# Shared stage of an attention and mixture-of-experts kernel: routed rows added inside the group, its own product added block by block, the held token group moved to second place, and its first loads issued earlier

## The chip, the cores and the metric

The kernel runs on one core of one Trainium2 chip. The metric is the device time of one execution in microseconds (us), lower is better. The kernel before takes 2059.78 us (median of three runs, 2058.6 to 2061.94).

## The reference

The input `x` is 16 x 256 x 512 float32: 16 batches of 256 tokens with 512 features. A masked attention layer with 8 heads makes a tensor of the same shape, and a feed-forward layer with experts works on its rows, 4096 tokens in all. Cut to what matters for this change:

```
x = x + _L0_ffn_ref(_L0_cond_ref(x, cond_2048, Wq, Wo), ...)

def _L0_ffn_ref(x, gate_w, w_gate, w_up, w_down, sw_gate, sw_up, sw_down, shared_gate_w):
    E, K = (8, 2); I = 352; IS = 1408
    top_w, top_i = jax.lax.top_k(softmax(x @ gate_w.T), K)
    moe_out = sum over the 2 chosen experts of top_w * ((silu(x @ w_gate) * (x @ w_up)) @ w_down)
    sh = silu(x @ sw_gate) * (x @ sw_up)
    shared_out = sh @ sw_down
    return moe_out + shared_out * sigmoid(x @ shared_gate_w)
```

So each of the 4096 output rows is the input row, plus two routed rows with their weights, plus the row of the shared expert times its gate.

## The kernel before

The program has three stages, each a block of its own with a barrier of all engines between them. Every engine's instruction order is written out by hand, and semaphores tie the engines together; an engine works strictly in order, and SyncE (SP in the profile) issues nearly all DMAs, also in order. Full float32 products are made of three fast ones: each operand is split into a high and a low part (ScalarE makes the high part, VectorE the low one), and three matmuls add up high x high, high x low and low x high.

**Attention** writes its rows to `attn` in HBM, and the router's logits to SBUF. This change leaves it alone.

**Experts** (`experts`) begins with the up part of the shared expert for tokens 0 to 511, the *held* group. For t = 0 to 10 (11 slices of 128 of the 1408 hidden features) SP loads a slice of the weights (`load_up`), TensorE makes gate and up, and SP stores the result to `held` (line 755). VectorE sorts the tokens by expert in the meantime. Then each of the 8 experts works through its tiles of 256 slots: GpSimd gathers the rows (`gather`, line 826), TensorE turns them and makes gate and up (line 1138) and down (line 1150), ScalarE copies the result to `y` (line 901) and SP stores it to `routed` (line 769). SP loads the raw weights of expert 0 at the start, those of expert 1 with `load(1)` after the last `held` store, and later ones two experts ahead (lines 733 to 735). ScalarE splits the weights of expert 1 (`split(1, ...)`, line 846) before it takes up the first tile of expert 0, so the SiLU of that tile stands behind `load(1)`. When its loop is over SP issues `load_ahead` for the next stage (one DMA of 1024 KB for 512 rows of `attn`, six of 256 KB for the first two weight slices), waits for the last routed store, and goes to the barrier.

**Shared** (`shared`) works on groups of 512 tokens in four blocks of 128 rows. Groups 0 to 6 are tokens 512 to 4095, and the held group comes last. A full group has 11 steps t: gate and up products (`up`, line 1456, 12 matmuls each), SiLU, h split into halves (lines 1388, 1390), and `down` (line 1467, 12 matmuls into the four banks `ps_y`), one step behind. The rows of the next group are turned by TensorE (`turn`, line 1450) in the last step. The held group needs no gate and up: its 11 steps are a load of h from `held` into one of two buffers `h_up` (line 1295), two splits (lines 1402, 1404) and `down`. In group 0 each step also splits a weight slice (lines 1341 to 1342 and 1371 to 1373), and SP loads the slices two steps ahead (lines 1171, 1172).

The output of a block is put together in `total[s]`, which SP fills with the residual rows of `x` (line 1281). `add_down` (line 1419) adds the shared product when all of the group's products are done; `add_chosen` (lines 1427, 1430) then adds the two routed rows, in steps 0 to 3 of the *next* group, and SP stores the block (line 1285). The routed rows come through `chosen`, two pairs of buffers: GpSimd gathers those of block b (line 1326, two indirect DMAs) when block b - 2 is finished. After the last group `add_chosen` runs by itself. GpSimd also makes the stage's own identity matrix `ident` (lines 1309, 1311), for which TensorE waits at the start.

Of the kernel before, what the change touches and what calls it, by code (L numbers as in the profile page):

```python
# [586 lines left out]
def experts(nc, ctx, sems, keep, attn, w_gate, w_up, w_down, sw_gate, sw_up, held, routed):  # L587
# [7 lines left out]
    P = 128  # L595
# [24 lines left out]
    ident = sb("ident", [P, P], f32)  # L620
# [12 lines left out]
    y = sb("y", [P, SB, H], f32)  # L633
# [42 lines left out]
    y_done, stored = sem("y_done"), sem("stored")  # L676
# [53 lines left out]
    def _(sp):  # L730
# [444 lines left out]
def shared(nc, ctx, sems, keep, x, attn, sw_gate, sw_up, sw_down, held, routed, out):  # L1175
# [12 lines left out]
    HELD = 1  # L1188
    NG = NTOK // GT - HELD
    TOPK = 2  # L1190

# [9 lines left out]
    ident = sb("ident", [P, P], f32)  # L1201
# [9 lines left out]
    h_up = [sb(f"h_up{n}", [P, GT], f32) for n in range(2)]  # L1211
    h_in = [sem(f"h_in{n}") for n in range(2)]
# [4 lines left out]
    base, consts = sem("base"), sem("consts")  # L1217
# [3 lines left out]
    t_mm, g_mm, u_mm, y_mm = sem("t_mm"), sem("g_mm"), sem("u_mm"), sem("y_mm")  # L1221
    xhi_done, xlo_done = sem("xhi_done"), sem("xlo_done")
    silu_done, h_done, hhi_done, h_split = sem("silu_done"), sem("h_done"), sem("hhi_done"), sem("h_split")
    slot_done, scale_done, y_read, sum_done, out_ready = sem("slot_done"), sem("scale_done"), sem("y_read"), sem("sum_done"), sem("out_ready")
# [15 lines left out]
    def groups(eng, group):  # L1240

        group(0)
        with eng.Fori(1, NG - 1) as g:
            group(g)
        group(NG - 1)

    def more(g):
        return not isinstance(g, int) or g + 1 < NG

    def rows_of(g, s):  # L1250

        return (GB * (g + HELD) + s) * P if not isinstance(g, int) or g < NG else s * P

    def blocks_of(g):

        return bass.ds(GB * (g + HELD), GB) if not isinstance(g, int) or g < NG else slice(0, GB)

# [3 lines left out]
    def _(sp):  # L1261

        for t in range(2, NI):

            sp.wait_ge(w_lo, 2 * (t - 1))
            load_chunk(sp, keep["ahead"], sw_gate, sw_up, sw_down, t)

        def group(g):
            if more(g):

                sp.wait_ge(t_mm, HT * (g + 1))
                load_rows(sp, keep["ahead"], attn, g + 1 + HELD)
            if not isinstance(g, int) or g:
                store(g - 1)
            for s in range(GB):
                load_residual(g, s)

        def load_residual(g, s):

            upto(sp, stored[s], 16 * g)  # L1280
            sp.dma_start(total[s][:], x_v[bass.ds(rows_of(g, s), P), :]).then_inc(residual_in[s], 16)  # L1281

        def store_block(g, s):
            sp.wait_ge(out_ready, GB * g + s + 1)
            sp.dma_start(out_v[bass.ds(rows_of(g, s), P), :], total[s][:]).then_inc(stored[s], 16)

        def store(g):
            for s in range(GB):
                store_block(g, s)

        def load_held(t):
            if t >= 2:

                sp.wait_ge(h_split, NI * NG + t - 1)
            sp.dma_start(h_up[t % 2][:], held[t * P:(t + 1) * P, :]).then_inc(h_in[t % 2], 16)

        groups(sp, group)
        for t in range(NI):
            load_held(t)
            if 0 <= t - 2 < GB:  # L1300
                store_block(NG - 1, t - 2)
                load_residual(NG, t - 2)
# [273 lines left out]
```

## Time and profile before

| | |
|---|---|
| median of 3 runs | 2059.78 us |
| the profiled execution's own time | 2059.99 us |
| its span, first to last instruction | 2058.2 us |
| TensorE busy | 1922.2 us, 93% of the span |
| VectorE busy | 1082.7 us, 53% |
| ScalarE busy | 709.4 us, 34% |
| GpSimd busy | 620.0 us, 30% |
| mean granted TensorE clock | 0.964 of full speed |
| DMA | 195.83 MB, mean 95 GB/s |

The stages in time: attention to about 735 us, the up part of the held group to about 834, experts to about 1335, shared to the end. PE is TensorE's matmuls, PEld its weight loads, DVE VectorE, ACT ScalarE, POOL GpSimd and SPq SyncE's DMA issues. The share of busy time is an average over the three stages; what a change in one stage is worth is read from the waits in it. The granted clock has two levels, 1.00 (2.4 GHz) and 0.50 (1.2 GHz).

### The profile page before, as it was taken

What the parts mean: (1) busy time and instruction counts of PE and PEld (TensorE: products, weight loads), DVE (VectorE), ACT (ScalarE), POOL (GpSimd) and SP (SyncE); (2) the same over time, 40 slices, a digit from 0 to 9 for tenths busy, and PEclk for the clock granted to TensorE, in tenths of its full rate; (3) what the DMA queues carried; (4) which work ended last, traced back from release to release, by engine and by line L of the source; (5) the groups of instructions that cost most, each with busy time, mean ns of one, the idle gap of its engine ahead of it and who ended that gap; (6) DMA issues with size and microseconds to landing.
All of it is one profiled execution on the core that took longest, in us unless ns stands there. A gap on an engine that the chain in (4) does not pass through costs nothing. (4 is left out here: it accounts for less than half of the span.)

```text
span 2058.2 us, 30150 instructions
## 1 busy us (share of the span) xinstructions
PE 1922.2 (93%) x10324; PEld 1416.7 (69%) x10325; DVE 1082.7 (53%) x1723; ACT 709.4 (34%) x1276; POOL 620.0 (30%) x444
## 2 busy tenths in 40 slices
PE   4999999999999869899999999979999999999995
PEld 2444444444444347799999999868888888888874
DVE  3788878887888548443444433343423323242334
ACT  1566666666666623232333332231010101011000
POOL 3556566666665526211111111100101001010101
PEclk6899999999999969999999999989999999999998
DMA  7776767676765063422333232162302112130204
GB/s 125 111 115 100 111 96 130 101 108 98 128 90 73 21 226 97 150 91 100 124 124 111 83 115 82 67 182 73 102 21 82 41 61 66 36 102 0 93 26 143
DMA packets 117831, 195.83 MB, mean 95 GB/s; under 512 B 11264, under 2 KB 43008, under 8 KB 117776
## 3 DMA queue, kind: packets, MB, share of 16 engines
q1 hardware_dynamic: 106736, 158.94, 34.4%
q0 software_dynamic: 11040, 36.18, 6.1%
q8 instruction: 31, 0.51, 0.1%
q14 instruction: 24, 0.20, 0.0%
HBM read 100.68 MB, written 43.25 MB: 70 GB/s over the span
## 5 line engine op out<-in xcount | busy, mean ns | idle before, releaser
L420 DVE TENSOR_REDUCE maxcol<-ps_m 128x1 f32<-128x512 f32 x512 | 336.9, 681 | 138.5 <-PE ps_m L562 133.4
L337 ACT ACTIVATE e<-ps_e 128x512 f32<-128x512 f32 x512 | 297.3, 596 | 186.5 <-PE ps_e L557 185.7
L148 POOL TENSOR_TENSOR e<-e 128x2048 f32<-128x2048 f32 x64 | 225.6, 3524 | 179.0 <-ACT e L337 178.9
L1384 DVE TENSOR_TENSOR s_h_f<-s_silu,s_ps_u 128x512 f32<-128x512 f32 x77 | 52.9, 688 | 393.5 <-PE s_ps_u L1456 344.0
L562 PE MATMUL ps_m<-kside,qside 97*128 97x512 f32 x512 | 224.3, 443 | 34.7 <-DVE maxcol L420 19.1
L1326 POOL DMA_INDIRECT s_chosen<-routed,s_slot_now x64 | 61.6, 962 | 620.9 <-DVE s_total L1430 609.6
L557 PE MATMUL ps_e<-qside,kside 98*128 98x512 f32 x512 | 236.8, 465 | 3.3 <-ACT e L337 2.1
L557 PEld LDWEIGHTS ps_e<-qside,kside 98*128 98x128 f32 x512 | 96.8, 190 | 191.8 <-ACT e L337 158.7
L1352 ACT ACTIVATE s_silu<-s_ps_g 128x512 f32<-128x512 f32 x77 | 46.0, 598 | 528.8 <-PE s_ps_g L1456 521.3
L1053 DVE TENSOR_TENSOR e_h_f<-e_silu,e_ps_h 128x256 f32<-128x256 f32 (+1 forms) x108 | 45.2, 418 | 250.1 <-ACT e_silu L894 250.1
L562 PEld LDWEIGHTS ps_m<-kside,qside 97*128 97x128 f32 x512 | 101.1, 197 | 80.6 <-DVE maxcol L420 54.6
L1467 PE MATMUL s_ps_y<-s_d_hi,s_h_hi 128*128 128x512 f32 x352 | 140.0, 398 | 10.2 <-DVE s_h_lo L1404 10.2
L1467 PE MATMUL s_ps_y<-s_d_lo,s_h_hi 128*128 128x512 f32 x352 | 138.7, 394 | 0.0
L1467 PE MATMUL s_ps_y<-s_d_hi,s_h_lo 128*128 128x512 f32 x352 | 138.7, 394 | 0.0
L455 PE MATMUL ps_num<-e,v 128*32 128x512 f32 x1024 | 138.0, 611 | 0.1
L386 DVE RECIPROCAL den<-den 128x128 f32<-128x128 f32 x128 | 119.5, 940 | 15.4 <-ACT den L268 15.4
L1456 PE MATMUL s_ps_g<-s_x_hi,s_gu_hi 128*128 128x512 f32 x308 | 121.3, 394 | 3.7 <-DVE s_d_lo L1373 3.6
L1138 PE MATMUL e_ps_h<-e_x_hi,e_hi_g 128*128 128x256 f32 (+1 forms) x432 | 122.0, 282 | 1.7 <-DVE e_x_lo L917 1.7
L1138 PE MATMUL e_ps_h<-e_x_lo,e_hi_u 128*128 128x256 f32 (+1 forms) x432 | 121.9, 282 | 0.0
L1138 PE MATMUL e_ps_h<-e_x_lo,e_hi_g 128*128 128x256 f32 (+1 forms) x432 | 121.9, 282 | 0.0
L1138 PE MATMUL e_ps_h<-e_x_hi,e_lo_g 128*128 128x256 f32 (+1 forms) x432 | 121.8, 282 | 0.0
L1138 PE MATMUL e_ps_h<-e_x_hi,e_hi_u 128*128 128x256 f32 (+1 forms) x432 | 121.6, 281 | 0.0
(233 smaller groups left out, 4189.0 us busy)
## 6 DMA issues: line engine op xcount, KB each, us to landing
routed<-e_y SPq DMA_DIRECT2D x36, 512.0 KB, 2.8
kside<-q_hi SPq DMA_DIRECT2D x64, 256.0 KB
qside<-qm_hi SPq DMA_DIRECT2D x64, 256.0 KB
x_f<-in_x SPq DMA_DIRECT2D x16, 512.0 KB, 3.5
kside<-q_lo SPq DMA_DIRECT2D x32, 256.0 KB
qside<-qm_lo SPq DMA_DIRECT2D x32, 256.0 KB
attn<-xo SPq DMA_DIRECT2D x32, 256.0 KB, 3.4
keep_rows<-attn SPq DMA_DIRECT2D x8, 1024.0 KB, 5.6
```

Source lines behind the costliest of these rows:

```text
L148: eng.tensor_tensor(into, into, e[k + 1][:, heads, :], ALU.add).then_inc(done, 1)
L337: act.activation(e[kb][:, g, :], ps_e[g % 2][:, :], ACT.Exp, scale=SCALE).then_inc(e_done, 1)
L386: dve.reciprocal(den[par][:, c], den[par][:, c]).then_inc(rd_done, 1)
L420: dve.reduce_max(maxcol[par][:, g * KB + kb:g * KB + kb + 1], ps_m[g % 2][:, :], AX.X).then_inc(max_done, 1)
L455: last = nc.tensor.matmul(ps_num[g * DK:(g + 1) * DK, :], v[n % RING][:, kb, g, :], e[kb][:, g, :], start=(kb == 0), stop=(kb == KB - 1))
L557: nc.tensor.matmul(ps_e[g % 2][:, :], kside[n][:, g, cols], qside[n][:, g, :], start=True, stop=True).then_inc(e_mm, 1)
L562: nc.tensor.matmul(ps_m[g % 2][:, :], qside[s2][0:MAXROW, g, cols], kside[s2][0:MAXROW, g, :], start=True, stop=True).then_inc(m_mm, 1)
L1138: last = nc.tensor.matmul(ps_h[t][0:width, k, :], l[k][:, m, at:at + width], r[:, m, :], start=(c == 0), stop=(c == len(terms) - 1))
L1326: pool.indirect_dma_start(out=chosen[k][s % 2][:], out_offset=None, in_=routed, in_offset=bass.IndirectOffsetOnAxis(ap=slot_now[:, k, s:s ...
L1384: dve.tensor_tensor(h_f[:], silu[:], ps_u[:], ALU.mult).then_inc(h_done, 1)
L1456: last = nc.tensor.matmul(ps[:], l[:, t, k, m, :], r[:, m, :], start=(c == 0), stop=(c == len(terms) - 1))
L1467: last = nc.tensor.matmul(ps_y[s][:], l[t % 2][:, c], r[:, t, :], start=(t == 0 and m == 0), stop=(t == NI - 1 and m == 2))
```

## The change

- The held group is at place 1, after one full group (tokens 512 to 1023), and six full groups follow. The function `places` sets this order for all engines. Its h goes through three buffers, two of which are the two halves of `y`, the buffer of the experts' results, which is now kept alive.
- `add_chosen` runs in steps 5 to 8 of the group's own 11 steps (`ADD_AT` = 5), before the shared product is there; a new semaphore `chosen_used` frees the `chosen` buffers. `add_down` comes at the end, block by block: TensorE signals each of the first three blocks by `y_last`, and the store of a block follows it.
- The copies of the weights (`scales`) stand at the start of a group.
- SP issues `load_ahead` before `load(1)` in the experts stage, right after the last `held` store. At the end of that stage SP does not wait for the routed stores any more; GpSimd does so at the start of the shared stage, before the first gather.
- In the shared stage SP issues the loads for the second full group's rows, the residual rows and the first three held slices after weight slice 3, before slice 4. The order before had rows and residual behind slice 10.
- `ident` is made once, in the experts stage.

The core of the diff:

```diff
@@ experts, SyncE
             sp.wait_ge(a_h_done, t + 1)
             sp.dma_start(held[t * P:(t + 1) * P, :], a_h[t % 2][:]).then_inc(a_stored[t % 2], 16)
+        sp.wait_ge(a_wlo, SI)
+        sp.wait_ge(a_t_mm, HT)
+        keep["load_ahead"](sp)
         sp.wait_ge(lo_done, NPARTS)
         load(1)
...
         each_expert(sp, start, tile)
-        total = sp.value_load(keep["bounds"][0:1, NE:NE + 1], min_val=1, max_val=NTILES - 1)
         for n in range(2):
             sp.wait_ge(a_stored[n], 16 * ((SI - n + 1) // 2))
-        keep["load_ahead"](sp)
-        alone(sp, stored, 16 * total + 16, consts, 8)
@@ shared
+    ADD_AT = NI - GB - 2
...
+    RING = 3
+    y = keep["ahead"]["y"]
+    h_up = [y[:, 0, :], y[:, 1, :], sb("h_up", [P, GT], f32)[:]]
...
+    def places(eng, group, held_group, alone_too=0):
 
         group(0)
-        with eng.Fori(1, NG - 1) as g:
-            group(g)
+        held_group()
+        for p in range(HELD_AT + 1, HELD_AT + 1 + alone_too):
+            group(p)
+        with eng.Fori(HELD_AT + 1 + alone_too, NG - 1) as p:
+            group(p)
         group(NG - 1)
@@ shared, SyncE
+        def exchange(p):
+            for s in range(GB):
+                if not isinstance(p, int) or p:
+                    store_block(p - 1, s)
+            for s in range(GB):
+                load_residual(p, s)
+
+        def load_held(t):
+            if t >= RING:
+
+                sp.wait_ge(h_split, NI * HELD_AT + t - RING + 1)
+            sp.dma_start(h_up[t % RING], held[t * P:(t + 1) * P, :]).then_inc(h_in[t % RING], 16)
...
+        def group_held():
+            exchange(HELD_AT)
+            for t in range(RING, NI):
+                load_held(t)
+
         for t in range(2, NI):
 
             sp.wait_ge(w_lo, 2 * (t - 1))
             load_chunk(sp, keep["ahead"], sw_gate, sw_up, sw_down, t)
...
+            if t == 3:
+                group(0)
+                sp.wait_ge(slot_done, 1)
+                for k in range(RING):
+                    load_held(k)
@@ shared, GpSimd
-        pool.memset(ident[:], 0.0).then_inc(base, 1)
-        pool.wait_ge(base, 1)
-        pool.affine_select(out=ident[:], in_=ident[:], compare_op=ALU.not_equal, fill=1.0, base=0,
-                           pattern=[[-1, P]], channel_multiplier=1).then_inc(consts, 1)
...
+        written = pool.value_load(keep["bounds"][0:1, NE:NE + 1], min_val=1, max_val=keep["tiles"] - 1)
+        alone(pool, keep["routed_stored"], 16 * written + 16, t_mm, 1)
...
-                    alone(pool, out_ready, b - 1, consts, 1)
+                    alone(pool, chosen_used, b - 1, slot_done, 1)
@@ shared, VectorE
+        def add_down(p):
+
+            dve.wait_ge(chosen_used, GB * (p + 1))
+            for s in range(GB):
+                if s < GB - 1:
+                    dve.wait_ge(y_last, (GB - 1) * p + s + 1)
+                else:
+                    dve.wait_ge(y_mm, NI * (p + 1))
+                dve.scalar_tensor_tensor(out=total[s][:], in0=ps_y[s][:], scalar=scale_now[:, TOPK, s:s + 1],
+                                         in1=total[s][:], op0=ALU.mult, op1=ALU.add).then_inc(out_ready, 1)
...
+        def group_held():
+            scales(HELD_AT)
+            for t in range(NI):
+                dve.wait_ge(h_in[t % RING], 16 * (t // RING + 1))
+                halves(HELD_AT, t, h_up[t % RING])
+                if ADD_AT <= t < ADD_AT + GB:
+                    add_chosen(HELD_AT, t - ADD_AT)
+            add_down(HELD_AT)
@@ shared, TensorE
-        pe.wait_ge(consts, 1)
...
+                if t == NI - 1 and s < GB - 1:
+                    last.then_inc(y_last, 1)
             last.then_inc(y_mm, 1)
```

**How the order moves, at three places.** On SP in the experts stage, between the last stores of `held` and the weights of expert 1 (`e_raw_*`), one piece of the difference (+ is the change):

```order
 L755 DMA held<-e_a_h 128x512 x3
+L1163 DMA keep_rows<-attn 128x4x512
+L1171 DMA keep_raw_gu<-in_sw_gate 128x4x128
+L1171 DMA keep_raw_gu<-in_sw_up 128x4x128
+L1172 DMA keep_raw_d<-in_sw_down 128x512
+L1171 DMA keep_raw_gu<-in_sw_gate 128x4x128
+L1171 DMA keep_raw_gu<-in_sw_up 128x4x128
+L1172 DMA keep_raw_d<-in_sw_down 128x512
 L733 DMA e_raw_g<-in_w_gate 128x4x352
 L733 DMA e_raw_u<-in_w_up 128x4x352
```

Seven DMAs of the next stage now stand ahead of `load(1)`; before, nothing did.

On SP in the shared stage of the change, between weight slices 3 and 4 (`keep_y` and `s_h_up` are the three held buffers, `s_total` the residual):

```order
L1171 DMA keep_raw_gu<-in_sw_up 128x4x128
L1172 DMA keep_raw_d<-in_sw_down 128x512
L1163 DMA keep_rows<-attn 128x4x512 [waits s_t_mm]
L1273 DMA s_total<-in_x 128x512 x4
L1290 DMA keep_y<-held 128x512 [waits s_slot_done]
L1290 DMA keep_y<-held 128x512
L1290 DMA s_h_up<-held 128x512
L1171 DMA keep_raw_gu<-in_sw_gate 128x4x128 [waits s_w_lo]
```

Eight DMAs, 2816 KB, now stand ahead of slice 4; before, slice 4 followed slice 3 at once.

On VectorE, the end of the program; before:

```order
L1419 SCALAR_TENSOR_TENSOR s_total<-s_ps_y,s_scale_now,s_total 128x512 [waits s_residual_in3]
L1427 SCALAR_TENSOR_TENSOR s_total<-s_chosen,s_scale_now,s_total 128x512 [waits s_y_read,s_chosen_in0]
L1430 SCALAR_TENSOR_TENSOR s_total<-s_chosen,s_scale_now,s_total 128x512 [waits s_sum_done]
L1427 SCALAR_TENSOR_TENSOR s_total<-s_chosen,s_scale_now,s_total 128x512 [waits s_y_read,s_chosen_in1]
L1430 SCALAR_TENSOR_TENSOR s_total<-s_chosen,s_scale_now,s_total 128x512 [waits s_sum_done]
L1548 UNCONDITIONAL_BRANCH
```

and in the change:

```order
L1391 CAST s_h_hi<-s_h_f 128x512 [waits s_y_mm,s_h_done]
L1393 TENSOR_TENSOR s_h_lo<-s_h_f,s_h_hi 128x512 [waits s_hhi_done]
L1422 SCALAR_TENSOR_TENSOR s_total<-s_ps_y,s_scale_now,s_total 128x512 [waits s_y_last,s_chosen_used]
L1422 SCALAR_TENSOR_TENSOR s_total<-s_ps_y,s_scale_now,s_total 128x512 [waits s_y_last] x2
L1422 SCALAR_TENSOR_TENSOR s_total<-s_ps_y,s_scale_now,s_total 128x512 [waits s_y_mm]
L1574 UNCONDITIONAL_BRANCH
```

The eight additions of routed rows (two for each block) that followed the last product are gone from the end, and only one addition waits for the very last product (`s_y_mm`).

## Rows read from the trace of the kernel before

**Rows 1.** The page: busy time, share of the span and instructions of each engine.

```profile
PE 1922.2 (93%) x10324; PEld 1416.7 (69%) x10325; DVE 1082.7 (53%) x1723; ACT 709.4 (34%) x1276; POOL 620.0 (30%) x444
```

**Rows 2.** Chain that ended last: the last down step of full groups; start, us, what.

```profile
1522.68 2.72 PE s_ps_y L1467 x12
...
1890.11 2.72 PE s_ps_y L1467 x12
```

**Rows 3.** Busy time by stretch: us, each engine, granted clock, DMA share, GB/s.

```profile
1538.40:1630.00 91.60, 91.60 (x412) 75.68 (x412) 30.89 (x51) 8.86 (x15) 7.86 (x9) 1.00 0.17 56
...
1995.50:2041.40 45.90, 35.65 (x133) 27.71 (x132) 20.76 (x36) 0.00 (x0) 8.76 (x9) 0.89 0.44 143
2041.40:2058.20 16.80, 0.03 (x1) 0.00 (x0) 8.56 (x12) 0.00 (x0) 4.05 (x4) 0.61 0.39 125
```

**Rows 4.** Timeline of SP and POOL at the end of experts: start, us, [idle before <-releaser].

```profile
1336.13 0.37 SPq L769 DMA_DIRECT2D routed<-e_y  x1
1337.32 0.40 SPq L1163 DMA_DIRECT2D keep_rows<-attn  x1
...
1341.53 1.59 SPq L1172 DMA_DIRECT2D keep_raw_d<-in_sw_down  x1
...
1343.71 0.21 POOL L1309 MEMSET s_ident<- 128x128 f32 x1 [22.82 <-POOLq L1546]
```

**Rows 5.** Timeline of PE from there to the first product of shared.

```profile
1344.43 1.97 PE L1450 MATMUL s_ps_t<-s_ident,keep_rows 128*128 128x128 f32 x8 [9.11 <-POOL s_ident L1311]
...
1352.51 0.76 PE L1456 MATMUL s_ps_g<-s_x_hi,s_gu_hi 128*128 128x512 f32 x1 [3.58 <-DVE s_d_lo L1373]
```

**Rows 6.** Timeline of SP, ACT and PE at the start of expert 0, around `load(1)`.

```profile
833.81 0.44 SPq L733 DMA_DIRECT2D e_raw_g<-in_w_gate  x1
...
844.44 1.38 ACT L846 ACTIVATE e_hi_g<-e_raw_g 128x1408 fp32r<-128x1408 f32 x1 [8.35 <-DMA e_raw_d<-in_w_down]
...
852.00 0.79 PE L1150 MATMUL e_ps_y<-e_hi_d,e_h_hi 128*128 128x512 f32 x1 [3.85 <-DVE e_h_lo L1057]
```

**Rows 7.** Busy time by stretch: `load(1)` moving, `load_ahead` moving.

```profile
837.00:840.00 3.00, 2.94 (x14) 2.95 (x14) 0.00 (x0) 0.00 (x0) 1.40 (x2) 0.50 1.07 393
...
1337.20:1346.00 8.80, 1.57 (x8) 1.57 (x8) 0.00 (x0) 0.42 (x1) 1.62 (x4) 0.58 1.04 309
```

**Rows 8.** A load behind a full queue at the start of experts; the zero fills' landing (DMA list).

```profile
753.33 1.17 SPq L739 DMA_DIRECT2D keep_raw_gu<-in_sw_gate  x1
...
764.63 1.06 ACT L861 ACTIVATE e_hi_g<-keep_raw_gu 128x1024 fp32r<-128x1024 f32 x1 [8.73 <-DMA keep_raw_gu<-in_sw_up]
...
routed<-e_zeros SPq DMA_DIRECT2D x9, 512.0 KB, 10.8
```

**Rows 9.** Group 0 of shared: ACT around weight slice 4.

```profile
1365.77 1.06 ACT L1341 ACTIVATE s_gu_hi<-keep_raw_gu 128x1024 fp32r<-128x1024 f32 x1 [2.33 <-DMA keep_raw_d<-in_sw_down]
...
1371.00 0.60 ACT L1352 ACTIVATE s_silu<-s_ps_g 128x512 f32<-128x512 f32 x1 [3.65 <-PE s_ps_g L1456]
```

**Rows 10.** The held group: waits of PE, VectorE's steps, the gather.

```profile
1999.50 0.50 PE L1467 MATMUL s_ps_y<-s_d_hi,s_h_hi 128*128 128x512 f32 x1 [3.93 <-DVE s_h_lo L1404]
...
1998.30 0.42 DVE L1402 CAST s_h_hi<-s_h_up 128x512 fp32r<-128x512 f32 x1
...
2000.14 0.75 DVE L1430 SCALAR_TENSOR_TENSOR s_total<-s_chosen,s_scale_now,s_total 128x512 f32<-128x512 f32 x1
...
2007.75 0.75 DVE L1427 SCALAR_TENSOR_TENSOR s_total<-s_chosen,s_scale_now,s_total 128x512 f32<-128x512 f32 x1 [2.58 <-DMA s_chosen<-routed,s_slot_now]
```

**Rows 11.** VectorE after the last product of group 0, and at the end of the program.

```profile
1446.63 2.73 DVE L1419 SCALAR_TENSOR_TENSOR s_total<-s_ps_y,s_scale_now,s_total 128x512 f32<-128x512 f32 x4 [1.35 <-issue]
...
2041.53 2.73 DVE L1419 SCALAR_TENSOR_TENSOR s_total<-s_ps_y,s_scale_now,s_total 128x512 f32<-128x512 f32 x4 [4.12 <-issue]
...
2054.96 0.75 DVE L1430 SCALAR_TENSOR_TENSOR s_total<-s_chosen,s_scale_now,s_total 128x512 f32<-128x512 f32 x1
```

**Rows 12.** DMA list, residual rows: KB each, median us from issue to landing.

```profile
s_total<-in_x SPq DMA_DIRECT2D x32, 256.0 KB, 4.3
```

More of the change, by code:

```diff
@@ L1238, in alone, with more, full, tokens @@
         eng.wait_ge(s, value)
-    def groups(eng, group):
+    def places(eng, group, held_group, alone_too=0):
         group(0)
-        with eng.Fori(1, NG - 1) as g:
-            group(g)
-        group(NG - 1)
[L1247 to L1256, printed above, removed]
+        held_group()
[3 more added lines that the diff above has]
+            group(p)
+        group(NG - 1)
+    def more(p):
+        return not isinstance(p, int) or p + 1 < NG
+    def full(p):
+        return 0 if isinstance(p, int) and p == 0 else p - 1
+    def tokens(p):
+        return {0: HELD_AT, HELD_AT: 0}.get(p, p) if isinstance(p, int) else p
     block = ctx.enter_context(nc.Block())
@@ L1266, in _ @@
             load_chunk(sp, keep["ahead"], sw_gate, sw_up, sw_down, t)
[L1268 to L1302, printed above, removed]
-        store(NG)
+            if t == 3:
[3 more added lines that the diff above has]
+                    load_held(k)
+        places(sp, lambda p: None if isinstance(p, int) and p == 0 else group(p), group_held, 1)
         for s in range(GB):
-            sp.wait_ge(stored[s], 16 * (NG + 1))
+            store_block(NG - 1, s)
@@ L1342, in split, with group @@
             act.activation(d_hi[:, t], raw_d[t % 2][:], ACT.Copy).then_inc(w_hi, 1)
-        def group(g):
-            first = isinstance(g, int) and g == 0
+        def group(p):
+            first = isinstance(p, int) and p == 0
+            f = full(p)
             for t in range(NI):
@@ L1373, in split @@
             dve.tensor_tensor(d_lo[:, t], raw_d[t % 2][:], d_hi[:, t], ALU.subtract).then_inc(w_lo, 1)
-        def group(g):
-            first = isinstance(g, int) and g == 0
-            for t in range(NI):
-                if first and t + 2 < NI:
-                    split(t + 2)
-                n = NI * g + t
-                dve.wait_ge(silu_done, n + 1)
-                dve.wait_ge(u_mm, n + 1)
-                upto(dve, h_split, n)
-                dve.tensor_tensor(h_f[:], silu[:], ps_u[:], ALU.mult).then_inc(h_done, 1)
-                dve.wait_ge(h_done, n + 1)
-                upto(dve, y_mm, n if t == 0 else n - 1)
-                dve.tensor_copy(h_hi[t % 2][:], h_f[:]).then_inc(hhi_done, 1)
-                dve.wait_ge(hhi_done, n + 1)
-                dve.tensor_tensor(h_lo[t % 2][:], h_f[:], h_hi[t % 2][:], ALU.subtract).then_inc(h_split, 1)
-                if t < GB and (not isinstance(g, int) or g):
-                    add_chosen(g - 1, t)
-            if more(g):
-                x_low(g + 1)
-            add_down(g)
@@ L1435, in _, with turn @@
         split(1)
-        groups(dve, group)
-        group_held()
-        for s in range(GB):
-            add_chosen(NG, s)
+        places(dve, group, group_held)
     @block.tensor
     def _(pe):
-        pe.wait_ge(consts, 1)
-        def turn(g, m):
+        def turn(f, m):
             if m == 0:
-                pe.wait_ge(rows_in, 16 * (g + 1))
-            upto(pe, xlo_done, HT * g + m - 1)
+                pe.wait_ge(rows_in, 16 * (f + 1))
+            upto(pe, xlo_done, HT * f + m - 1)
             for s in range(GB):
```

178 lines of the change are left out of this document (103 added, 75 removed).

## The prediction

> **What bounds the kernel now.** I read the page first: TensorE is busy 93% of the span, no other engine over 53% [rows 1], so what counts is where PE waits or runs at half clock. The chain of waits then shows the shared stage's full groups: the same down step recurs four groups later after 1890.11 - 1522.68 = 367.43 us, 91.86 us for each, without a gap [rows 2], and the stretch table has such a stretch filled, at granted clock 1.00 and a DMA share of 0.17 [rows 3]. Nothing is to be had there. The same table shows two stretches where PE is not filled: the held group, 45.90 us with 35.65 busy at clock 0.89, and 16.80 us behind it with no product at all [rows 3]. The timelines add two places. Between experts and shared PE idles 9.11 us until `ident` is made, and waits again before its first product [rows 5]; GpSimd makes `ident` only when SP, last at the barrier, has issued its seven loads [rows 4]. And at the start of expert 0, PE idles 3.85 us because ScalarE stood 8.35 us waiting for `load(1)` [rows 6]. That one is not a target of the change, but a moved step runs into it.
>
> **a. Seven loads ahead of `load(1)`.** They are 1024 + 6 x 256 = 2560 KB, 2.62 MB. `load(1)` began at 833.81 and its last piece released ScalarE at 844.44 [rows 6], 10.6 us, and in the middle of it the DMA engines were full and moved 393 GB/s [rows 7]. So time ahead of it is not absorbed: ScalarE splits expert 1's weights before the first SiLU of expert 0, VectorE's h stands behind that, PE's down behind h, and after 852.00 PE has no slack up to the end of the stage. The delay passes on one to one. Price: the same seven loads moved at 309 GB/s, a store included [rows 7], 2.62 MB / 309 = 8.5 us; at the 393 GB/s of `load(1)` it is 6.7 us. I take the middle, **+7.6 us**. Lower bound 4: the 6.4 us of a slightly better rate, less some of the half-clock time that PE has after its wait anyway. Upper bound 10.5: a weight slice that met a full queue released ScalarE at 764.63 after its issue at 753.33, 11.3 us, of which a DMA alone needs a part [rows 8]. The row shows that a load behind others lands late; it does not show that the queue is served in order. The Trainium skill, "DMA: Bandwidth & Descriptors", section "Queues, rings and completion order", says that each DMA engine consumes a queue's descriptors in ring order, which speaks against this part of the change. By its fabric ceiling of 435 GB/s ("Specifications") the term would be an estimated 6.0 us and the sum 1.6 us lower; the measured rates decide here.
>
> **b. From experts to shared.** SP's last store is issued by 1336.13 + 0.37 = 1336.50. Before, it went on to load, and its last issue ended at 1341.53 + 1.59 = 1343.12; GpSimd started 0.59 after [rows 4]. Now SP leaves the loop (at most the 0.8 us that lay before 1337.32) and reaches the barrier near 1336.7; 0.6 us later every engine goes, and PE needs no `ident`. PE starts near 1337.3 instead of 1344.43, **-7.1 us** (bounds -7.5 and -5.8). The wait for the last routed store moves to GpSimd; queued behind it are the slot copy and the first gathers, which nobody needs before step 5. The held loads on SP wait for that copy, too, long after it is done. From the first turn to the first product 8.08 us pass [rows 5]; the chain of ScalarE and VectorE in it stays, its 16 turns ran at half clock and may be quicker after a shorter idle time: **-0.5** (0 to -1.5).
>
> **c. Group 0.** SP puts eight DMAs, 2816 KB or 2.88 MB, ahead of slice 4. At 309 to 393 GB/s they take 7.3 to 9.3 us from about the time that slice 3 is through. Slice 4 was in at 1365.77, and would now be in near 1370; ScalarE splits it (1.06 us and a smaller piece) before SiLU 2, which began at 1371.00 [rows 9], and PE asks for SiLU 2 only after an up and a down product, 5.4 us later. The cover is about 4 us: **0**, and up to +4 if it is gone, since later slices catch up.
>
> **d. The held group at place 1.** Before, from the end of the last full group (1995.6) to the last product (2041.5, when VectorE starts [rows 11]) it took 45.9 us [rows 3]. Now, counted from the end B of group 0: VectorE, idle for 1.35 us before group 0's additions after the low parts of the next rows, is free from about B - 1.4, so its four additions, 2.73 us, end near B + 1.4 [rows 11]; the scale copies take 0.25, and from a finished addition to the first product took 1.1 us (split at 1998.30, product at 1999.50 [rows 10]). PE waits 2.75 us where it waited 3.93. Then 11 steps of 2.72 = 29.9 us [rows 2]. Stalls on `held` should go: three slices are there, and slice 3 comes behind the last store (2.5 us) and the residual loads that wait for the stores, so it is issued near B + 4.5 and lands some 4.3 later, as a residual load does [rows 12], and is needed by B + 9.7. A new stall comes: blocks 0 and 2 share a pair of buffers, and from a finished block to the next gather's arrival 2000.9 to 2007.75 = 6.85 us passed [rows 10], while here only two steps, 5.44 us, lie between. VectorE waits 3 us in step 7, and PE about 1.5 us in step 8. With 0.85 us for one possible half-clock stretch the group takes 2.75 + 29.9 + 1.5 + 0.85 = 35.0: **-10.9 us**. Bounds: -12.5 if the gather is covered and the clock holds, -7 with one more wait like the 3.93.
>
> **e. The end.** Before, 16.7 us from the last product to the end of the span. Now three blocks are added while the last one is multiplied; after it come one addition (0.75, and 0.1 to start) and one store. The last addition before ended at 2054.96 + 0.75 = 2055.71, 2.5 us before the end [rows 11]; three stores just ahead cost 0.2. That is 3.5 us: **-13.2 us** (-13.6 to -12).
>
> **Costed at nothing:** `add_chosen` in steps 5 to 8 of full groups (two additions, 1.5 us, in a step of 8.16 where VectorE is busy a third of the time [rows 3]; gathers have 16 us); `y_last`, an increment on a product that exists; two more scale copies ahead of splits.
>
> **The sum:** 7.6 - 7.1 - 0.5 + 0 - 10.9 - 13.2 = -24.1 us. Against the profiled execution's 2059.99 us that gives 2035.9; it lay 0.2 above the median of the runs, so I forecast **2035.7 us**, 1.2% faster. The bounds are rarely bad together; the case's own range is 2031 to 2042.
>
> **Rivals.** (1) *The early loads cost nothing*: `load(1)` overtakes them, or the wait is hidden. For it: a part of the 10.6 us is issue and start, which may overlap. Against it: ScalarE's 8.35 us wait was on the path, with full engines. Term a goes, 2035.7 - 7.6 = 2028.1. (2) *The held group keeps its stalls*: SP's chain of stores, residual loads and held loads, or the gather, costs as much at place 1 as at the end. For it: both showed as waits there. Against it: three slices are loaded far ahead. Term d goes, 2046.6. (3) *The boundary does not shrink*, so the change does not do what it says: something other than SP and `ident` holds PE, a barrier or code. Term b goes, 2043.3. Against it: GpSimd started 0.59 us after SP's last issue. (4) *Slower*: `load(1)` is served far later than the rates say. Its place is ScalarE's split before expert 0's first SiLU, and it decides from a delay of 7.6 + 24.1 = 31.7 us, at which the 2.62 MB move at under 83 GB/s. The nearest row for such a price is the zero fills, 10.8 us for 512 KB [rows 8]; five times that is 54 us, which gives 2035.7 - 7.6 + 54 = 2082. Against it: these landed late because they stood in line behind each other, at full rate.
>
> **How the numbers follow.** Forecast 0.76, rival 1 0.10, rival 2 0.08, rival 3 0.04, rival 4 0.02. The range of 8 in 10 runs from rival 1 up to near rival 3, 2028 to 2043; left out are rivals 2 and 4 and the tails of the forecast. A measurement of this kernel tells 0.2%, some 4 us, from no change. All cases but rival 4 lie far below that, so faster 0.97, same 0.01, slower 0.02.
>
> **What would show it.** a: ScalarE's wait before `e_hi_g` at the start of expert 0 is near 16 us instead of 8.35, PE's behind it near 11. b: PE idles some 2 us between the stages, and no `ident` is made. c: no PE wait at SiLU in group 0. d: PE waits near 2.8 us at the held group's first product, about 1.5 in step 8, and not on `held`. e: about 3.5 us from the last product to the end. The forecast is wrong if ScalarE's wait stays at 8 us, if PE waits on held slices at place 1, or if group 0 is longer than before.

## The result, and the profile after

The change takes the kernel from 2060.39 us (median of four runs, the three above and one more, 2058.6 to 2061.94) to **2045.47 us** (median of four, 2045.07 to 2046.97). The ratio is 0.9929, with a 95% interval of 0.9912 to 0.9946: 0.7% faster. The forecast was 2035.7 with a range of 2028 to 2043, so the direction was right, the gain was 14.9 us where 24.1 were forecast, and the time lies 2.5 us above the range. The profiled execution took 2045.46 us with a span of 2043.7, 14.5 below the span before.

The page after hardly differs from the one before [rows 1]:

```profile
PE 1920.0 (94%) x10324; PEld 1415.8 (69%) x10325; DVE 1080.5 (53%) x1723; ACT 709.3 (35%) x1276; POOL 619.9 (30%) x442
```

TensorE has the same work, and what changed are its idle and half-clock stretches. So the reading goes through the five places of the prediction. Timelines give the start, the duration, the instruction, and in brackets the idle time before it with its releaser.

**a, experts.** ScalarE and PE at the start of expert 0 (before: 8.35 and 3.85 us, [rows 6]):

```profile
855.27 1.38 ACT L846 ACTIVATE e_hi_g<-e_raw_g 128x1408 fp32r<-128x1408 f32 x1 [17.87 <-DMA e_raw_d<-in_w_down]
```
```profile
862.83 0.79 PE L1150 MATMUL e_ps_y<-e_hi_d,e_h_hi 128*128 128x512 f32 x1 [14.78 <-DVE e_h_lo L1057]
```

ScalarE waits 9.5 us longer and PE 10.9. From the first turn of expert 0 to the last product of the stage it took 501.08 us before (834.24 to 1335.32), and now 510.20 (835.56 to 1345.76): **+9.1**, with +7.6 forecast. The profiles of the runs below bear this out: in the six that have the seven loads ahead of `load(1)`, this one included, the stage takes 509.4 to 510.6 us, and in the four that have none ahead 498.9 to 501.1, on average 10.1 less. One pair is good to about a microsecond. SP shows why ScalarE waits:

```profile
835.21 0.38 SPq L1163 DMA_DIRECT2D keep_rows<-attn  x1
...
839.76 1.52 SPq L1172 DMA_DIRECT2D keep_raw_d<-in_sw_down  x1
841.33 0.44 SPq L733 DMA_DIRECT2D e_raw_g<-in_w_gate  x1
...
845.34 0.47 SPq L735 DMA_DIRECT2D e_raw_d<-in_w_down  x1
```

The seven early loads occupy SP from 835.21 to 841.28, and `load(1)` follows. Of `load(1)` the last piece is issued by 845.81 and in at 855.27. So 6.1 of the 9.5 us pass before `load(1)` is even issued. The stretch table shows the DMA engines full the whole time, and the DMA list has 1.05 MB of gathers by GpSimd in it beside the loads (columns: the stretch, its length, the busy time of PE, PEld, DVE, ACT and POOL, the granted clock, the DMA share, GB/s):

```profile
835.60:855.30 19.70, 10.73 (x88) 10.26 (x88) 1.29 (x2) 1.11 (x3) 4.21 (x6) 0.87 0.97 310
```

**b, the boundary.** PE idles 1.88 us where it idled 9.11 [rows 5]: **-7.2**, with -7.1 forecast.

```profile
1347.64 1.06 PE L1467 MATMUL s_ps_t<-keep_ident,keep_rows 128*128 128x128 f32 x8 [1.88 <-PEq L1572]
...
1355.23 0.76 PE L1473 MATMUL s_ps_g<-s_x_hi,s_gu_hi 128*128 128x512 f32 x1 [3.58 <-DVE s_d_lo L1385]
```

From the first turn to the first product it is 7.59 us where it was 8.08, the forecast **-0.5**, and for the reason that it named: the first eight turns take 1.06 us where they took 1.97 [rows 5]. All eight profiles with 1.9 us of idle time have 7.6 us here, and the three with 4.8 us or more have 8.1.

**c, group 0.** From its first product to its end 95.81 us pass, before 94.04: **+1.8**, with 0 forecast. ScalarE waited 6.91 us for weight slice 2 (before 5.10) and 7.88 for slice 4 (before 2.33, [rows 9]). Only the first of these reaches PE. ScalarE before, its wait for slice 2, and then ScalarE and PE in the change:

```profile
1357.59 1.06 ACT L1341 ACTIVATE s_gu_hi<-keep_raw_gu 128x1024 fp32r<-128x1024 f32 x1 [5.10 <-DMA keep_raw_d<-in_sw_down]
```
```profile
1362.12 1.06 ACT L1352 ACTIVATE s_gu_hi<-keep_raw_gu 128x1024 fp32r<-128x1024 f32 x1 [6.91 <-DMA keep_raw_d<-in_sw_down]
1364.41 1.06 ACT L1352 ACTIVATE s_gu_hi<-keep_raw_gu 128x1024 fp32r<-128x1024 f32 x1 [0.23 <-DMA keep_raw_d<-in_sw_down]
1367.35 0.60 ACT L1364 ACTIVATE s_silu<-s_ps_g 128x512 f32<-128x512 f32 x1 [1.35 <-PE s_ps_g L1473]
1375.83 1.06 ACT L1352 ACTIVATE s_gu_hi<-keep_raw_gu 128x1024 fp32r<-128x1024 f32 x1 [7.88 <-DMA keep_raw_d<-in_sw_down]
```
```profile
1364.32 0.47 PE L1473 MATMUL s_ps_g<-s_x_hi,s_gu_hi 128*128 128x512 f32 x1 [1.67 <-ACT s_silu L1364]
```

**d, the held group** runs from 1451.04 to 1491.26, 40.2 us where it took 45.9 [rows 3]: **-5.7**, with -10.9 forecast. PE waits three times, never for `held`:

```profile
1453.79 0.50 PE L1484 MATMUL s_ps_y<-s_d_hi,s_h_hi 128*128 128x512 f32 x1 [2.75 <-DVE s_h_lo L1393]
1477.90 0.50 PE L1484 MATMUL s_ps_y<-s_d_hi,s_h_hi 128*128 128x512 f32 x1 [0.43 <-DVE s_h_lo L1393]
1483.88 0.50 PE L1484 MATMUL s_ps_y<-s_d_hi,s_h_hi 128*128 128x512 f32 x1 [2.95 <-DVE s_h_lo L1393]
```

and runs at half clock after the first and the third wait (1.00 would be 2.4 GHz, 0.50 is 1.2 GHz):

```profile
1451.00:1491.30 40.30, 34.17 (x134) 27.18 (x134) 21.39 (x38) 0.00 (x0) 8.71 (x9) 0.92 0.59 186
1454.70:1457.70 3.00, 3.00 (x8) 2.30 (x7) 0.10 (x1) 0.00 (x0) 0.00 (x0) 0.50 0.96 307
1484.90:1488.20 3.30, 3.30 (x10) 2.54 (x9) 0.07 (x1) 0.00 (x0) 2.18 (x3) 0.53 0.68 192
```

Its 11 steps are 29.9 us at full clock [rows 2]. PE was busy for 34.17, so the clock cost 4.3, some 2 for each stretch; the other 6.1 are the waits, 2.75 + 0.43 + 2.95. Behind the second and the third wait stands VectorE, which waits for gathered rows (L1408 adds the first of the two rows of a block):

```profile
1470.49 0.75 DVE L1408 SCALAR_TENSOR_TENSOR s_total<-s_chosen,s_scale_now,s_total 128x512 f32<-128x512 f32 x1
1471.27 0.75 DVE L1411 SCALAR_TENSOR_TENSOR s_total<-s_chosen,s_scale_now,s_total 128x512 f32<-128x512 f32 x1
1475.25 0.75 DVE L1408 SCALAR_TENSOR_TENSOR s_total<-s_chosen,s_scale_now,s_total 128x512 f32<-128x512 f32 x1 [1.95 <-DMA s_chosen<-routed,s_slot_now]
1476.03 0.75 DVE L1411 SCALAR_TENSOR_TENSOR s_total<-s_chosen,s_scale_now,s_total 128x512 f32<-128x512 f32 x1
1481.22 0.75 DVE L1408 SCALAR_TENSOR_TENSOR s_total<-s_chosen,s_scale_now,s_total 128x512 f32<-128x512 f32 x1 [3.37 <-DMA s_chosen<-routed,s_slot_now]
```

Block 0 is added by 1469.30 and block 2's rows are in at 1475.25, 5.95 us later. Block 1 is added by 1472.02 and block 3's rows are in at 1481.22, **9.2 us** later, though it is the same pair of gathers. GpSimd issues them directly one after the other, and SP issues the 1024 KB of rows for the next group in the same moment:

```profile
1472.36 1.03 POOL L1338 DMA_INDIRECT s_chosen<-routed,s_slot_now  x1 [0.30 <-DVE s_total L1411]
1473.69 0.94 POOL L1338 DMA_INDIRECT s_chosen<-routed,s_slot_now  x1 [0.30 <-issue]
```
```profile
1473.69 0.43 SPq L1163 DMA_DIRECT2D keep_rows<-attn  x1
```

It was no single event: in the six profiles that keep these steps and this row load, block 2's rows take 5.9 to 6.2 us and block 3's 9.0 to 10.2, PE's third wait is 2.6 to 3.7 us, and a half-clock stretch follows it each time.

**e, the end.** VectorE's four additions (before [rows 11]) now overlap the last products, and 3.4 us lie between the last product at 2040.3 and the end, before 16.8: **-13.4** beside -13.2 forecast.

```profile
2038.36 2.73 DVE L1422 SCALAR_TENSOR_TENSOR s_total<-s_ps_y,s_scale_now,s_total 128x512 f32<-128x512 f32 x4 [1.54 <-PE s_ps_y L1484]
```

The six full groups take 549.04 us beside 549.1 before. Expert 0's first turn came 1.3 us later, which the change isn't shown to cause: in its own profile and those of its eight variants, whose edits lie behind that point, the turn lies between 833.9 and 838.3. The sum: 1.3 + 9.1 - 7.2 - 0.5 + 1.8 - 5.7 - 13.4 = -14.6, the span's -14.5. The 9.6 us by which the forecast's -24.1 missed it are, in order of size, **d 5.2, c 1.8, a 1.5, the start 1.3**.

### The profile page after: what moved, and what is told of

Its sections match the earlier page's. It is cut to its first block and busy times, and to the rows that moved or that the text cites. A ratio compares the mean times of both kernels' runs of the same rounds, so it can differ in the third digit from the quotient of the medians.

```text
span 2043.7 us, 30248 instructions
## 1 busy us (share of the span) xinstructions
PE 1920.0 (94%) x10324; PEld 1415.8 (69%) x10325; DVE 1080.5 (53%) x1723; ACT 709.3 (35%) x1276; POOL 619.9 (30%) x442
## 3 DMA queue, kind: packets, MB, share of 16 engines
q1 hardware_dynamic: 106736, 158.94, 34.6%
## 5 line engine op out<-in xcount | busy, mean ns | idle before, releaser
L823 POOL COPY e_now<-e_token_of 128x2 uint32 (+1 forms) x37 | 7.2, 195 | 384.3 <-PE e_ps_t L1121 383.0
```

## The experiments

Unless said otherwise each is an edit of the changed kernel. Runs with one time have no interval; in those the trace at the place of the edit decides, not the total.

### Is the wait at expert 0 a matter of the order of SP's loads?

```diff
             sp.dma_start(held[t * P:(t + 1) * P, :], a_h[t % 2][:]).then_inc(a_stored[t % 2], 16)
+        sp.wait_ge(lo_done, NPARTS)
+        load(1)
         sp.wait_ge(a_wlo, SI)
         sp.wait_ge(a_t_mm, HT)
         keep["load_ahead"](sp)
-        sp.wait_ge(lo_done, NPARTS)
-        load(1)
```

> The changed kernel with load(1) issued before the seven early loads, everything else as in the change. Theory A (the seven loads delay load(1) by the time that their 2.62 MB take on the DMA engines, and that reaches TensorE one to one): ScalarE's wait before expert 1's split falls from 17.87 us back to about 8.4, TensorE's from 14.78 to about 3.9, and the kernel is 9.1 us faster than the change, near 2036.4. Theory B (the experts stage began 1.3 us late and the rest is the warm-up of the clock or another cause, not the place of the loads): less than 3 us gained. Theory C (whatever is second in the queue pays: the seven loads collide with the gathers and the loads of expert 2): TensorE's wait shrinks by 11 us, but part of it comes back within the experts stage or at its end.

Measured: 2035.55 us (median of four, 2033.65 to 2036.63), ratio to before 0.9879 (0.9862 to 0.9895). Timelines of ScalarE and of PE:

```profile
847.85 1.38 ACT L846 ACTIVATE e_hi_g<-e_raw_g 128x1408 fp32r<-128x1408 f32 x1 [8.62 <-DMA e_raw_d<-in_w_down]
```
```profile
855.40 0.79 PE L1150 MATMUL e_ps_y<-e_hi_d,e_h_hi 128*128 128x512 f32 x1 [5.54 <-DVE e_h_lo L1057]
```

ScalarE's wait is back at 8.6 us, though the same 2.62 MB now follow right behind `load(1)`, and the experts take 500.4 us (837.38 to 1337.78), 9.8 less than in the change. The total is 9.9 less, so nothing of it comes back elsewhere, as theory C had it. The boundary idle stays at 1.88. So the whole of a comes from the loads that stand ahead of `load(1)`; loaded behind it they are hidden, and b is kept.

### Which of the seven loads costs what?

Here only the 1024 KB of rows are ahead of `load(1)`, and the six weight loads behind it:

```diff
-        keep["load_ahead"](sp)
+        keep["rows_ahead"](sp)
         sp.wait_ge(lo_done, NPARTS)
         load(1)
+        keep["load_ahead"](sp)
```

> The changed kernel with only one of the seven loads, the rows (1024 KB, 1.05 MB), ahead of load(1), and the six weight loads (1536 KB) behind it. Theory A by bytes: TensorE's wait at expert 0 rises by 1.05 / 2.62 of the 10.9 us that it rose by, so it is near 8.2 us (3.85 + 4.4) instead of 14.78. Theory A by issue: a DMA's cost is its issue time on SyncE (0.4 us for the rows, 5.7 for the six), so the wait is near 4.5 us. If the 512-byte lines of the weight slices are the slow part, the rows cost 1.05 MB / 393 GB/s = 2.7 us and the wait is near 6.5.

Measured: 2040.85 us (one run). PE (one line further down than in the change):

```profile
838.26 1.09 PE L1122 MATMUL e_ps_t<-keep_ident,e_rows 128*128 128x128 f32 x8 [1.72 <-DMA e_rows<-attn,e_now]
...
859.13 0.79 PE L1151 MATMUL e_ps_y<-e_hi_d,e_h_hi 128*128 128x512 f32 x1 [6.88 <-DVE e_h_lo L1058]
```

PE's wait of 6.88 us lies nearest the 6.5 that the text above has for slow short lines. But the wait also takes in how fast PE ran before it, so the time from the first turn to the product after the wait is the better measure. It is 20.87 us here, 27.27 in the change, and 18.02 in the run before, with nothing ahead of `load(1)`. By these three profiles the rows (1.05 MB) cost 2.85 us and the six weight loads (1.57 MB) 6.4. Theory A by issue falls, since the rows take SP 0.4 us to issue.

Whether short lines make the weight loads slower (four of the six have lines of 512 bytes, the other two and the rows of 2048) isn't shown. The same time lies between 16.45 and 18.02 us in the four profiles with nothing ahead and between 26.47 and 27.39 in the six with all seven. Held against these, the rows cost 2.9 to 4.4 us (237 to 368 GB/s) and the weight loads 5.6 to 6.5 (241 to 281 GB/s), which overlap. From average to average it is 9.7 us for all seven, of which the rows take 3.6, and their share by bytes would be 3.9.

### What delays block 3's gather?

SP's load of the next rows waits until the routed rows of the held group are added:

```diff
                 sp.wait_ge(t_mm, HT * (full(p) + 1))
+                if isinstance(p, int) and p == HELD_AT + 1:
+                    sp.wait_ge(chosen_used, GB * (HELD_AT + 1))
                 load_rows(sp, keep["ahead"], attn, tokens(p + 1 if not isinstance(p, int) or p else HELD_AT + 1))
```

> The changed kernel with the load of the rows for the third full group held back on SyncE until the held group's routed rows are added. Theory D (block 3's gather, 9.2 us from a free buffer to its rows, is slow because that 1024 KB load was issued at the same time and shares the DMA engines): VectorE's wait of 3.37 us for it falls below 1 us, TensorE's wait of 2.95 us in the held group and the half-clock stretch behind it go, and the held group takes some 4 us less than its 40.2. Theory E (the two gathers of a pair of blocks stand behind each other on GpSimd and at the DMA, whatever else runs): the wait stays within 1 us of 2.95.

Measured: 2039.87 us (one run). VectorE:

```profile
1470.31 0.75 DVE L1413 SCALAR_TENSOR_TENSOR s_total<-s_chosen,s_scale_now,s_total 128x512 f32<-128x512 f32 x1
1474.55 0.76 DVE L1410 SCALAR_TENSOR_TENSOR s_total<-s_chosen,s_scale_now,s_total 128x512 f32<-128x512 f32 x1 [2.22 <-DMA s_chosen<-routed,s_slot_now]
1475.34 0.75 DVE L1413 SCALAR_TENSOR_TENSOR s_total<-s_chosen,s_scale_now,s_total 128x512 f32<-128x512 f32 x1
1477.08 0.75 DVE L1410 SCALAR_TENSOR_TENSOR s_total<-s_chosen,s_scale_now,s_total 128x512 f32<-128x512 f32 x1
```

Block 1 is added by 1471.06, block 3's rows are there without a wait at 1477.08, at most 6.0 us later, where it was 9.2. PE keeps its first wait and 0.70 us in step 8; the 2.95 us and the half-clock stretch behind it are gone. The group takes 35.6 us:

```profile
1450.11:1485.70 35.59, 32.14 (x133) 26.17 (x134) 21.22 (x37) 0.00 (x0) 8.79 (x9) 0.95 0.62 201
```

That is 4.6 us less than in the change: 2.7 in waits and 1.9 in clock. So the row load delays block 3's gather, and theory E falls. That 35.6 lies near the forecast's 35.0 is in part luck: the later wait is 0.70 us where 1.5 were forecast, and the one half-clock stretch costs 2.2 where 0.85 were.

### Or can the gather be given more time?

The four additions of the held group go into steps 3, 4, 8 and 9 instead of 5 to 8, so that five steps and not two lie between a pair of buffers' release and its next use. The row load stays where the change has it:

```diff
-                if ADD_AT <= t < ADD_AT + GB:
-                    add_chosen(HELD_AT, t - ADD_AT)
+                if t in (3, 4, 8, 9):
+                    add_chosen(HELD_AT, (3, 4, 8, 9).index(t))
```

> The changed kernel with the held group's routed rows added in steps 3, 4, 8 and 9 instead of 5, 6, 7 and 8. Both D and E: from block 0's addition to block 2's lie five steps, 13.6 us, more than the 9.2 us of the slower gather, so TensorE's waits of 0.43 and 2.95 us in the held group and the half-clock stretch behind them go, and the group takes 40.2 - 3.4 - 1.6 = 35.2 us. If the residual rows are not there by step 3, a wait for them in step 3 takes part of it back.

Measured: 2037.63 us (one run). The only wait left in the group is the one at its start, and the clock holds:

```profile
1453.21 0.50 PE L1484 MATMUL s_ps_y<-s_d_hi,s_h_hi 128*128 128x512 f32 x1 [2.74 <-DVE s_h_lo L1393]
```
```profile
1450.47:1483.40 32.93, 30.19 (x133) 25.01 (x134) 21.22 (x37) 0.00 (x0) 9.14 (x9) 1.00 0.68 224
```

32.9 us, 7.3 less than in the change. Of the 2.7 us between this and the run before, 0.7 are the wait in step 8; the rest is clock (30.19 busy against 32.14), and most of it came behind the wait at the group's start, 2.75 us in both, after which the clock fell in the one run and held in the other. So about 2 us of this are no effect of the edit. PE is busy for 30.19 us with no half-clock stretch, 32.14 with one and 34.17 with two.

### What makes the new wait in group 0?

First the transfers ahead of slice 4, two slices later:

```diff
-            if t == 3:
+            if t == 5:
                 group(0)
```

> The changed kernel with weight slices 4 and 5 issued before the eight loads (rows, residual, held) of SyncE's first group, instead of behind them. Theory F (TensorE's 1.67 us wait at the first SiLU of group 0 comes from those eight DMAs): the wait goes. Theory G (it comes from the four gathers, which now start 2.6 us after TensorE instead of together with it and run into slices 2 and 3): the wait stays between 0.6 and 1.7 us, ScalarE's wait for slice 4, 7.88 us, falls back to about 2.3, and since slice 4 was covered anyway, the kernel's time is within 1.5 us of the change's.

Measured: 2045.15 us (one run). ScalarE's wait for slice 4 falls from 7.88 to 0.48 us, and yet nothing is gained: PE's wait at SiLU is 2.25 us, ScalarE's for slice 2 is 7.39, and group 0 takes 97.9 us, 2.1 more than in the change. (The total comes out level since the clock held at the start of this run's held group.) So slice 4 was covered, as c had it, and the eight loads alone don't make the 1.8 us. Next the first gathers, held back until weight slice 2 is through:

```diff
             pool.wait_ge(slot_done, p + 1)
+            if isinstance(p, int) and p == 0:
+                pool.wait_ge(w_lo, 6)
```

> The changed kernel with the gathers of group 0 held back until weight slice 2 is split. Theory G: slices 2 and 3 have the DMA engines to themselves, ScalarE's wait for slice 2 falls from 6.91 us to about 4.5, TensorE's wait of 1.67 us at the first SiLU goes, group 0 is 1.7 us shorter. Theory F: the wait stays. The gathers now meet the eight loads and slice 4, whose cover was 3 us; if that is used up, a new wait at the third SiLU appears.

Measured: 2044.10 us (one run). PE's wait is 0.86 us, ScalarE's for slice 2 6.13, and group 0 takes 95.0, 0.8 less than in the change. ScalarE's wait for slice 4 grows to 9.60, and no wait at the third SiLU appears. That looks like an answer until it is held against the other six variants, which all have the early gathers and the eight loads: there the same PE wait is 0.58 to 1.11 us (0.81 with ScalarE's at 6.06). So the gathers alone aren't shown to be the cause either.

The wait itself is the change's, though. PE has it in all nine profiles of the change and its variants (0.58 to 2.25 us, ScalarE's for slice 2 5.5 to 7.5), and in neither profile of the kernel before, where ScalarE waits 4.7 and 5.1. Each suspect was taken away alone, never both together, so that either of them suffices isn't excluded. **Its cause stays open**, and c is worth 0.4 to 2.3 us (group 0 takes 94.4 to 96.4 in the eight profiles other than the run on slices 4 and 5).

### Is it SP's issuing that holds the boundary?

The seven loads back at the end of the experts stage, all else as in the change:

```diff
-        sp.wait_ge(a_wlo, SI)
-        sp.wait_ge(a_t_mm, HT)
-        keep["load_ahead"](sp)
         sp.wait_ge(lo_done, NPARTS)
         load(1)
...
             sp.wait_ge(a_stored[n], 16 * ((SI - n + 1) // 2))
+        keep["load_ahead"](sp)
```

> The changed kernel with the seven loads back at the end of the experts stage, identity matrix and the wait for the routed stores as in the change. Theory A: TensorE's wait at expert 0 is back near 4 to 5.5 us, 9 to 10 us gained there; at the boundary SyncE's 5.9 us of issue are back before the barrier, so TensorE idles about 1.9 + 6.6 = 8.5 us instead of 1.88. Net some 3 us faster than the change, near 2042. If SyncE's issue was not what held the barrier (rival 3 of the prediction), the idle time stays near 2 us and the kernel comes out near 2036.

Measured: 2037.10 us (one run). SP, and then PE (two lines further up):

```profile
1333.90 0.37 SPq L769 DMA_DIRECT2D routed<-keep_y  x1
1334.53 0.40 SPq L1161 DMA_DIRECT2D keep_rows<-attn  x1
...
1339.02 1.85 SPq L1170 DMA_DIRECT2D keep_raw_d<-in_sw_down  x1
```
```profile
1341.31 1.94 PE L1465 MATMUL s_ps_t<-keep_ident,keep_rows 128*128 128x128 f32 x8 [8.21 <-PEq L1570]
```

PE idles 8.21 us instead of 1.88 and starts 0.44 after SP's last issue, with no `ident` to wait for. The experts take 499.2 us, 11.0 less than in the change. So the early loads alone, in the place the change gives them, give 6.3 us at the boundary (and the 0.5 behind it) and take 11.0 at the start: **this part of the change costs more than it brings**. The total was expected near 2042 and came 5 lower: a is 11.0 here and not 9.1, the first turn came 1.65 earlier, and the held group took 1.7 less, since its first half-clock stretch did not come.

### The early loads without the rest of the change

This is the kernel *before* with only the seven loads moved ahead of `load(1)`. SP still waits for the routed stores at the end of the stage:

```diff
             sp.dma_start(held[t * P:(t + 1) * P, :], a_h[t % 2][:]).then_inc(a_stored[t % 2], 16)
+        sp.wait_ge(a_wlo, SI)
+        sp.wait_ge(a_t_mm, HT)
+        keep["load_ahead"](sp)
         sp.wait_ge(lo_done, NPARTS)
         load(1)
...
-        keep["load_ahead"](sp)
         alone(sp, stored, 16 * total + 16, consts, 8)
```

> The kernel before with one part of the change alone: the seven loads moved ahead of load(1). Everything else, the wait for the routed stores and the stage's own identity matrix included, stays. Theory A: TensorE's wait at expert 0 rises from 3.85 us to about 14, 9 to 10 us lost. At the boundary SyncE has no loads to issue, but still waits for the last routed store, which lands some 3 us after its issue, and GpSimd makes the identity matrix after that, so TensorE's idle time falls from 9.11 us only to about 5.5. Net some 6 us slower than the kernel before, near 2066: this part alone is a loss. If TensorE's wait at expert 0 depended on something else in the change, the kernel would be 3 to 4 us faster than before.

Measured: 2065.63 us (median of ten, 2063.27 to 2068.83) beside 2060.65 for the kernel before, ratio 1.0024 (1.0015 to 1.0034): **slower by 0.24%**, 5 us where 6 were forecast. PE's wait at expert 0 is 14.90 us, and at the boundary 4.81:

```profile
863.25 0.79 PE L1152 MATMUL e_ps_y<-e_hi_d,e_h_hi 128*128 128x512 f32 x1 [14.90 <-DVE e_h_lo L1059]
...
1350.54 1.97 PE L1452 MATMUL s_ps_t<-s_ident,keep_rows 128*128 128x128 f32 x8 [4.81 <-POOL s_ident L1313]
```

The boundary gives only 4.3 of its 9.11 us, since SP's last store is issued by 1346.91 and GpSimd makes `ident` only at 1349.82, 2.9 us later: the wait for that store, and the barrier. Moving this wait to GpSimd behind the barrier, and keeping `ident`, is what brings the idle time down to 1.88. No run separates the two; GpSimd starts `ident` 0.72 us before PE's first turn, so at least 2.2 of the 2.9 us between 4.81 and 1.88 are the wait.

### Both repairs together

`load(1)` ahead of the seven loads, and the additions in steps 3, 4, 8 and 9:

```diff
+        sp.wait_ge(lo_done, NPARTS)
+        load(1)
...
         keep["load_ahead"](sp)
-        sp.wait_ge(lo_done, NPARTS)
-        load(1)
...
-                if ADD_AT <= t < ADD_AT + GB:
-                    add_chosen(HELD_AT, t - ADD_AT)
+                if t in (3, 4, 8, 9):
+                    add_chosen(HELD_AT, (3, 4, 8, 9).index(t))
```

> The changed kernel with two repairs together: load(1) before the seven early loads, and the held group's routed rows added in steps 3, 4, 8 and 9. If the two costs are separate, their gains add up: 9.9 us (first run of that repair, 2045.5 to 2035.6) and 7.3 us (held group from 40.2 to 33.0 us), so near 2028.5, 1.5% below the kernel before. If the second depended on when the experts stage ended, less.

Measured: **2029.32 us** (median of four, 2028.31 to 2030.49), ratio to before 0.9853 (0.9837 to 0.987). It beats both kernels: 1.5% faster than before, and 16 us below the change. ScalarE's wait at expert 0 is 7.04 us, the boundary idle 1.87, and the held group, with one half-clock stretch, 34.6. The sum of the two gains (2028.5) came out, though not by its parts: the experts took 498.9 us, 1.5 less than in the first repair, and the held group 1.7 more than in the second.

## Why the prediction was right and wrong

- **a, +7.6 forecast, +9.1 measured.** The mechanism is shown, by order alone (`load(1)` first: 9.8 us back). The Trainium skill, "DMA: Bandwidth & Descriptors", section "Queues, rings and completion order", has each DMA engine work through a queue in ring order; the runs agree, with ScalarE's wait at 17.87 us behind the early loads and at 8.62 ahead of them. Mis-sized was the rate. I took the middle between 6.7 and 8.5 us. Spread over the 9.1 us that they added, the 2.62 MB make 288 GB/s, below both rates that I had; the engines moved 310 GB/s in that stretch, and part of it was gathers, for which the term had nothing. The lower of my rates, 309 GB/s, was measured on these very loads [rows 7] and would have given 8.5. Over all profiles the cost is about 10 us, near my upper bound of 10.5.
- **b, -7.1 and -0.5 forecast, -7.2 and -0.5 measured.** Right, and the loads-back run names SP's issue time as the holder. Rival 3 falls.
- **c, 0 forecast, +1.8 measured.** Slice 4 came 7.3 us later after the first product and not some 4, and the cover, which I had put at about 4, was larger and held. Another wait came, for slice 2, for which ScalarE had waited 5.1 us before too and which the prediction did not look at. Its cause is open.
- **d, -10.9 forecast, -5.7 measured: the step that failed.** The first wait (2.75) was exact, `held` stalled nowhere, and a wait for the gather in step 8 was foreseen. The step "from a finished block to the next gather's arrival 2000.9 to 2007.75 = 6.85 us passed" took one price for both pairs. It was 5.95 for block 2 and 9.2 for block 3, because the same change puts SP's 1024 KB row load for the next group beside it. That made waits of 3.4 us where 1.5 were in the sum (+1.9). The second term that failed is the clock: half clock cost 4.3 us where 0.85 were in the sum (+3.4). The 0.85 stood for one possible stretch, and no row shows that price. Two came and cost about 2 us each; the second came behind block 3's wait in all six profiles that have this wait, and the first, behind the group's start, in five of nine. Moving the row load brought the group to 35.6, and spreading the additions to 32.9. The price of 6.85 was read in the last group, where no next group's rows are loaded (the DMA share there was 0.80); the row was right and its surroundings weren't. The bound of -12.5 for a covered gather and a full clock was a slip, since 2.75 + 29.9 = 32.65 makes it -13.2. Rival 2 had the gather in it, as a stall of the old size; the group's gain of 5.7 lies about halfway between it and the forecast.
- **e, -13.2 forecast, -13.4 measured.** Right.
- **Rival 1** (the early loads are free) falls. **Rival 4** falls too: `load(1)` came some 10 us later, not 31.7 or 54. That the early loads alone make the kernel before 5 us slower is their transfer time, against the 4.3 us that they give back at the boundary there.
- **The range** took in each term's bounds but let them be "rarely bad together". Here a, c and d all lay on the bad side, and so did the start, which was no term of the sum; only d went beyond its bound (-5.7 against -7).

## What to carry to other kernels

When loads are moved earlier to clear one queue, ask what stands behind them in the same queue: put them behind the load that the critical path needs, and the gain at the old place is free; ahead of it, it cost more than it gave. A transfer's latency holds for the traffic that it was read in, so look at what the new order issues in the same microsecond, on the other queues too. A wait that can bring a stretch of half clock costs more than itself: here 3 us of waiting brought 2 us more. When a gather is too slow for its buffers, the order of use can be changed instead of the load: a shared buffer pair should have as many steps between release and use as the group allows.

## What the hardware showed unexpectedly

- The same pair of gathers landed 5.95 and 9.2 us after release, the latter with a 1024 KB load from another queue issued in the same moment; without that load it was at most 6.0. In all six profiles with that load it was 9.0 to 10.2.
- SP's time for issuing one DMA is no constant: in group 0 of the change the last DMA of weight slice 2 took it 0.50 us (`sw_down`, 1356.11), and the same of slice 4, behind the eight loads, 3.10 (1366.92).
- After the same wait of 2.74 to 2.77 us of PE at the start of the held group the granted clock fell to 0.50 for about 3 us in five profiles (the change, and the runs on `load(1)` first, late rows, late gathers and both repairs) and stayed at 1.00 in the four other variants of the change. At the same idle time before it, the half clock came or did not.
- With nothing left to issue, the stage boundary costs PE 1.88 us from its last product to the first turn of the next stage (1.87 or 1.88 in eight profiles). SP's last store is issued 1.18 after that product, and PE starts 0.70 after it.
